# Fifty-four one-column products behind the seven warm-up products that open TensorE's program

## What is computed

```python
x = x + tanh(g_xattn) * xattn(layernorm(x), ctx, ctx, Wq, Wk, Wv, Wo)   # 16 heads of 64, causal mask
x = x + tanh(g_ffn)   * ffn(layernorm(x), gamma1, Wq, bq, Wdown, ..., We)
# xattn: softmax(q k^T / 8, causal) v, then @ Wo
# ffn:   rmsnorm, per token an attention among 16 heads of 8 features, @ Wo,
#        rmsnorm, softmax gate over 8 experts, sum of gated h2 @ We[e], residuals
```

## Time and profile before

| | us |
|---|---|
| median of three executions | 279.35 (279.3 to 280.47) |
| the profiled execution, its own time | 278.05 |
| its span, from the first to the last instruction | 276.1 |
| TensorE busy, matmul | 236.9 (86% of the span) |
| TensorE busy, weight load | 165.5 (60%) |
| VectorE busy | 211.8 (77%) |
| GpSimd busy | 168.3 (61%) |
| ScalarE busy | 159.7 (58%) |
| mean granted TensorE clock | 0.956 of full speed |

### The profile page before, as it was taken

One profiled execution on the slowest core, in us unless ns is written; L12 is line 12 of the kernel. 1 busy time (PEld: TensorE's weight loads), 2 busy tenths in 40 slices (PEclk: granted clock), 3 DMA queues, 4 the chain that ended last, 5 costly groups with the idle time before them and its releaser, 6 DMA issues.

```text
span 276.1 us, 7648 instructions
## 1 busy us (share of the span) xinstructions
PE 236.9 (86%) x3118; PEld 165.5 (60%) x3118; DVE 211.8 (77%) x366; ACT 159.7 (58%) x432; POOL 168.3 (61%) x187
## 2 busy tenths in 40 slices
PE   7999979897999899989999999799999697752570
PEld 7765766856676676758585858575856373511130
DVE  0237543399999989998999727999999989999810
ACT  2546515463776767766686868546767464643431
POOL 4104042336488778777786665737878767888734
PEclk9999999999999999999999999999999799977757
DMA  6990000000000000000000000000000000000000
GB/s 207 366 278 7 0 4 2 2 1 5 0 2 10 2 13 2 11 4 12 2 2 10 5 9 0 15 0 2 4 9 2 11 2 12 1 10 12 0 10 10
DMA packets 6016, 7.28 MB, mean 26 GB/s; under 512 B 477, under 2 KB 4830, under 8 KB 5982
## 3 DMA queue, kind: packets, MB, share of 16 engines
q1 hardware_dynamic: 5550, 6.16, 7.0%
q10 hardware_dynamic: 432, 0.64, 0.6%
HBM read 5.88 MB, written 0.92 MB: 25 GB/s over the span
## 4 chain that ended last, share of the span: by engine, by line
PE 58%; DVE 29%; issue 7%; ACT 4%; POOL 1%; POOLq 0%; ACTq 0%; DVEq 0%
PE ps_a L664 36%; PE ps_c L664 9%; DVE oraw L562 6%; PE ps_b L664 6%; DVE ps_e L537 5%; PE ps_e L664 3%; DVE onorm L567 3%; DVE nmax L492 2%; DVE prod L551 2%; PE ps_b L716 2%; DVE prod L528 2%; DVE psums L497 2%; DVE fqkv L523 1%; PE ps_b L661 1%; DVE esum L550 1%
## 5 line engine op out<-in xcount | busy, mean ns | idle before, releaser
L252 POOL TENSOR_TENSOR probs<-probs,prinv 120x672 f32<-120x672 f32 x16 | 23.7, 1478 | 34.2 <-DVE prinv L501 34.0
L664 PE MATMUL ps_c<-fwe_sb,x2T 128*128 128x512 f32 x56 | 33.0, 722 | 5.7 <-DVE glog L578 5.7
L664 PE MATMUL ps_a<-aT,wo_sb 128*128 128x112 f32 x256 | 33.0, 281 | 2.6 <-ACT aT L361 1.3
L415 ACT ACTIVATE exb<-ps_c,gate 128x128 f32<-128x128 f32 x112 | 30.9, 394 | 5.1 <-POOL gate L310 2.8
L281 POOL TENSOR_TENSOR exb<-exb 128x640 f32<-128x640 f32 x14 | 21.6, 1543 | 20.0 <-ACT exb L415 20.0
L261 POOL TENSOR_TENSOR prod<-fqkv 128x1024 f32<-128x1024 f32 x14 | 33.1, 2365 | 0.7 <-DVE fqkv L523 0.7
L664 PEld LDWEIGHTS ps_a<-aT,wo_sb 128*128 128x128 f32 x256 | 29.9, 192 | 5.2 <-ACT aT L361 3.0
L537 DVE TENSOR_REDUCE ps_e<-prod 128x256 f32<-128x2048 f32 x14 | 32.0, 2285 | 0.0
L562 DVE TENSOR_REDUCE oraw<-prod 128x128 f32<-128x2048 f32 x14 | 31.4, 2242 | 0.0
L664 PE MATMUL ps_a<-wv_sb,cT 128*64 128x512 f32 x128 | 31.0, 605 | 0.0
L361 ACT COPY aT<-ps_a 128x448 f32<-128x448 f32 x32 | 15.5, 536 | 21.9 <-PE ps_a L664 21.9
(11 more groups left out here) (116 smaller groups left out, 459.4 us busy)
## 6 DMA issues: line engine op xcount, KB each, us to landing
xp_sb<-in_xp SPq DMA_DIRECT2D x1, 896.0 KB, 7.9
out<-out_sb SPq DMA_DIRECT2D x14, 64.0 KB, 1.5
xT<-in_x_t SPq DMA_DIRECT2D x1, 784.0 KB, 9.5
cT<-in_ctx_t SPq DMA_DIRECT2D x1, 784.0 KB, 11.0
wv_sb<-in_wv SPq DMA_DIRECT2D x1, 512.0 KB, 8.0
wo_sb<-in_wo SPq DMA_DIRECT2D x1, 512.0 KB, 12.6
fwe_sb<-in_fwe SPq DMA_DIRECT2D x1, 512.0 KB, 9.3
fw_sb<-in_fw SPq DMA_DIRECT2D x1, 266.0 KB, 12.3
```

The lines of the kernel that those rows point to most:

```text
L252: nc.gpsimd.tensor_tensor(pr[0:TG, NC:C, :, 0:S], pr[0:TG, NC:C, :, 0:S], prinv[p % 2][0:TG, NC:C, :].unsqueeze(3).to_broadcast([TG, C - N ...
L415: last = nc.scalar.activation(exb[f % 3][:, e, :], ps_c[:, half, e % 4 * D:(e % 4 + 1) * D], ACT.Copy, scale=gate[f % 2][:, e:e + 1])
L664: return nc.tensor.matmul(o, lhsT, rhs, start=start, stop=stop, skip_group_check=True)
```

## The change

Behind the seven warm-up products, and ahead of everything else that TensorE does, 54 more products are issued. Each has the same 128x128 identity as its weights and one column of it as the moving operand, and writes one column of the same bank of `ps_b`. Nobody reads the results, nothing waits for them by a semaphore, and nothing else is changed.

```diff
 WARM_UP = 7
+PHASE = 54
...
             for _n in range(WARM_UP):
                 nc.tensor.matmul(ps_b[:, 0, 0:128], ident[:, :], ident[:, :], start=True, stop=True)
+            for _n in range(PHASE):
+                nc.tensor.matmul(ps_b[:, 0, 0:1], ident[:, :], ident[:, 0:1], start=True, stop=True)
```

## The result

The changed kernel takes 301.49 us (median of four, 301.29 to 303.19) against 279.33 us; the ratio is 1.082, with a 95% interval of 1.074 to 1.090. It is slower, as forecast. The forecast was 300.3 us, the range 289.5 to 305.0. The profiled execution took 301.29 us with a span of 299.2 us, so the span grew by 23.1 us. By the medians the change costs 22.2 us.

What follows compares the result with a forecast made beforehand. The prediction took TensorE's chain at the head as setting the end: 19.8 us for 108 pairs plus 1.1 us at the key projections, 20.9 us on 279.35, gave 300.3 us, range 289.5 to 305.0.

Steps and rivals of the forecast that it cites:

- The path: At TensorE's head, anything between warm-up and key projections sets the end; only 0.03 us is open to hide products.
- The price of a pair: Each weight load plus matmul of the added products costs 0.11 us at full clock, 0.21 at the low one.
- The rival of cheap pairs: Added products at 0.016 us a pair, 1.7 us in all: 278.0 us with a better end, otherwise 281.1; chance 0.03.
- The clock: During the added products, one stretch of 3.4 us at full clock (31 pairs), then 77 pairs low: 19.8 us; chance 0.38.
- full clock throughout: Weight loads count as activity, so the clock rises near 6 us and stays through the added products: 291.0 us; chance 0.36.
- low throughout: Warm-up earns no stretch at full clock, so the added products cost 23.0 us: 303.5 us in all; chance 0.20.
- What comes behind: Key projections after the added products start at the low clock, losing net 0.8 to 1.4 us, taken as 1.1.
- the end open by 1.6 us: In the last steps, shifted low-clock stretches could change an expert group by up to 1.6 us each way; nothing in the middle.
- everything follows later by one amount: After the key projections all work shifts equally, by 20.9 us in the forecast; VectorE's row statistics start near 49 us.

Runs made afterwards that it cites:

- the 56 bfloat16 products: Kernel before, without the 54 products, plus 56 one-column bfloat16 products with 64x64 weights ahead of the scores of pair 0: 286.22 us, ratio 1.029.

## Why the prediction was right

*The path.* Right. The chain runs through the products without a gap on either side, and no other engine or transfer absorbed any of them: the centring products start 21.08 us later.

*The price of a pair.* Right: 0.11 us at full clock and 0.213 at the low one, and a quarter of the latter with a quarter of the weight columns. The rival of cheap pairs is out. By the load figure of the Trainium skill, which the prediction weighed, the sum was 11.6 us; 19.7 us were measured, so here the measurement decides: the pace follows the granted clock.

*The clock.* Right in kind, and in the profiled execution to the letter: one stretch at full clock, then low, 19.73 us against 19.8. With 64 and 128 streamed columns and loads as busy as here, the clock stayed full. That the warm-up earned one stretch at full clock was in part luck: with 27 products, and with weights of 32 columns, the same warm-up earned none. The rival "full clock throughout" described those kernels, 291.0 us forecast and 292 to 293 us measured. The rival "low throughout" may well be one of the changed kernel's own four executions, the one of 303.19 us, near that rival's 303.5. Its mean clock is 0.954, higher than the 0.919 of the profiled one, and that fits. A head that is low from the start has no clock on record and counts as full, as with 27 products, where the record begins at 19.68 us and the mean is 0.943. From the means I estimate (1 - 0.919) x 299.2 x 2 = 48.5 us of recorded low clock against (1 - 0.954) x 301.1 x 2 = 27.7. The difference of 20.8 us is near the 20.48 us from 8.59 us on that the profiled execution has on record as low. The execution has no trace in this case, so it stays an estimate.

*What comes behind.* 5.38 - 4.00 = 1.4 us for the key projections, at the upper end of 0.8 to 1.4, where I took 1.1. The products and this together are 19.73 + 1.38 = 21.1 us, against 20.9.

*The remaining 2.0 us.* This the prediction did not have. It kept the end open by 1.6 us for the clock in the last steps, but the end was not the place: the lateness was 23.23 us at the last `x1T` and 23.1 at the end. The step that failed is "everything follows later by one amount". Adding 216 instructions moved the borders of TensorE's blocks of instructions against the work. One stop of 1.37 us went, and one of 2.05 us came, with 1.0 us of low clock behind it; later stops changed by some tenths. Shown is that the stops stand only at borders of 256 instructions, that the borders move with the count alone, and that each stop ends 1.2 to 1.5 us behind the end of its block's packet. A border brings a stop where TensorE comes to it sooner than that. What sets the start of a packet stays open: it lies between 2.7 us before and 9.4 us after TensorE passes the border before, so the number of stops can't be forecast yet, and my counts for 27 products and for the 56 bfloat16 products were wrong.

## What to carry to other kernels

A product of one column is not a cheap product: here each paid for its full weight load, 0.11 us a pair at full clock and 0.213 at the low one, which most of them met. Filler that kept the clock here streamed 64 columns or more, and it gained time only where TensorE waited anyway. Ahead of the first real work, where the warm-up already ends with the data's arrival, each product cost its full time. In a kernel with long runs of short products even instructions that are nearly free can cost some us, so after any change of TensorE's instruction count look at its "issue" stops before explaining a difference of 1% by anything else.

## What was not expected of the hardware

The same 108 pairs of load and matmul took 13.1 us with 128 streamed columns and 19.7 us with one. TensorE's 25 stops, of 0.7 to 4.22 us, all stood 193 past a multiple of 256 instructions and ended 1.2 to 1.5 us behind a 16 KB packet on the instruction queue. Behind a stop of 2.05 us the clock was 0.50 for the next stretch, which cost another 1.0 us. Stops of 1.50 us at the same instruction came out both ways: with 64 columns the output projection behind it took 2.94 us, with 128 columns 2.04 us.
